# Two attention layers over one sparse graph: the adjacency turned into 8-bit floats by the transfers that load it

## The reference

```python
h = relu(layernorm(x))                          # x: 8192 x 128 f32
e = (h @ Ws) @ (h @ Wt).T                       # 8192 x 8192 scores
alpha = softmax(where(adj > 0, e, -9e15))       # adj: 8192 x 8192 int32, 0 or 1
x = x + alpha @ (h @ Wc)
h = relu(layernorm(x)); Wh = h @ W1
e = leaky_relu(s1[:, None] + s2[None, :], 0.2)  # s1 = Wh @ a1, s2 = Wh @ a2
x = x + elu(softmax(where(adj > 0, e, -9e15)) @ Wh)
```

## Time and profile before

| | |
|---|---|
| median of three runs | 1405.4 us |
| span of the profiled execution (its own time is not given beside it) | 1402.6 us |
| busy, share of the span | PE 91%, VectorE 89%, ScalarE 73%, GpSimd 2% |
| moved by DMA | 363.10 MB, of which the adjacency 268 MB |
| chain that ended last | PE 46%, DMA 18% (all of it the adjacency), VectorE 16%, "issue" 12% |

### The profile page before, as it was taken

One profiled execution on the slowest core, in us unless ns is written; L12 is line 12 of the kernel. 1 busy time (PEld: TensorE's weight loads), 2 busy tenths in 40 slices (PEclk: granted clock), 3 DMA queues, 4 the chain that ended last, 5 costly groups with the idle time before them and its releaser, 6 DMA issues.

```text
span 1402.6 us, 76097 instructions
## 1 busy us (share of the span) xinstructions
PE 1276.6 (91%) x31819; PEld 1131.9 (81%) x31947; DVE 1250.6 (89%) x2323; ACT 1024.8 (73%) x2036; POOL 32.3 (2%) x75
## 2 busy tenths in 40 slices
PE   5867899999999999999999999989899999999996
PEld 3656788888888888878878888877799999999995
DVE  8877799999999999989999999847899999999996
ACT  5755576767667677667676666748789999999994
POOL 2200000000000000000000000013000000000000
PEclk9979899999999999999999999999899999999998
DMA  6678899999999999999999999531134244334322
GB/s 249 248 266 287 280 345 369 370 381 368 368 391 357 377 378 366 383 380 341 382 378 361 376 374 374 223 114 55 56 108 121 81 124 123 108 94 123 117 85 72
DMA packets 104081, 363.10 MB, mean 259 GB/s; under 512 B 11520, under 2 KB 36352, under 8 KB 70144
## 3 DMA queue, kind: packets, MB, share of 16 engines
q1 hardware_dynamic: 103936, 361.02, 71.2%
HBM read 319.03 MB, written 41.94 MB: 257 GB/s over the span
## 4 chain that ended last, share of the span: by engine, by line
PE 46%; DMA 18%; DVE 16%; issue 12%; ACT 5%; SPq 1%; DVEq 1%; ACTq 0%; POOL 0%; POOLq 0%
DMA arena<-in_adjB 18%; PE ps L883 16%; PE ps L857 9%; DVE arena L1490 5%; PE ps L769 4%; DVE arena L1465 4%; PE ps L764 3%; PE ps L737 3%; DVE mx L1499 2%; ACT arena L1132 2%; PE ps L790 2%; PE ps L725 2%; PE ps L763 1%; PE ps L664 1%; SPq L434 1%
## 5 line engine op out<-in xcount | busy, mean ns | idle before, releaser
L790 PE MATMUL ps<-arena 128*128 128x129 f32 x2048 | 249.0, 280 | 0.4 <-issue 0.4
L1118 ACT ACTIVATE arena<-ps 128x512 f32<-128x512 f32 x256 | 153.2, 598 | 129.8 <-PE ps L737 129.8
L883 PE MATMUL ps<-arena 128*128 128x129 f32 x2048 | 245.1, 278 | 0.4 <-issue 0.4
L790 PEld LDWEIGHTS ps<-arena 128*128 128x128 f32 x2048 | 240.6, 196 | 0.6 <-issue 0.6
L1465 DVE TENSOR_SCALAR arena<-arena 128x2048 fp8e4<-128x2048 int32 x192 | 234.9, 1224 | 3.5 <-PE ps L752 1.5
L883 PEld LDWEIGHTS ps<-arena 128*128 128x128 f32 x2048 | 236.8, 194 | 0.5 <-issue 0.5
L1708 DVE TENSOR_SCALAR arena<-arena 128x128 f32<-128x128 f32 x768 | 202.4, 339 | 19.5 <-issue 14.3
L1112 ACT ACTIVATE arena<-ps 128x512 f16<-128x512 f32 x256 | 153.9, 601 | 52.5 <-PE ps L725 52.3
L769 PEld LDWEIGHTS ps<-arena 128*128 128x128 f16 x2048 | 137.5, 99 | 62.0 <-issue 2.2
L1499 DVE TENSOR_REDUCE mx<-ps 128x1 f32<-128x1024 f32 x128 | 155.7, 1216 | 29.9 <-PE ps L769 29.3
L737 PE MATMUL ps<-arena 128*32 128x128 f16 x8192 | 165.3, 223 | 16.5 <-issue 10.7
(11 more groups left out here) (165 smaller groups left out, 1400.4 us busy)
## 6 DMA issues: line engine op xcount, KB each, us to landing
arena<-in_adjB SPq DMA_DIRECT2D x256, 1024.0 KB, 7.3
sel_pick<-arena SPq DMA_DIRECT2D x64, 256.0 KB, 9.6
sel<-arena SPq DMA_DIRECT2D x64, 256.0 KB, 9.5
arena<-sel_pick SPq DMA_DIRECT2D x64, 256.0 KB, 3.8
arena<-sel SPq DMA_DIRECT2D x64, 256.0 KB, 2.8
arena<-in_xB SPq DMA_DIRECT2D x4, 1024.0 KB, 6.1
x_t<-in_x SPq DMA_DIRECT2D x64, 64.0 KB, 8.0
x_mid<-y_t SPq DMA_DIRECT2D x64, 64.0 KB, 8.3
```

The costliest lines, as they stand in the source:

```text
L790: last = nc.tensor.matmul(pv_ps, p_T[:, s * P:(s + 1) * P], v_sel[:, b, s, :], start=False, stop=(s == SB - 1), skip_group_check=True)
L883: last = nc.tensor.matmul(xv_ps[b], w_msk[:, b, s, :], x1_sel[:, b, s, 0:VW], start=False, stop=(s == SB - 1), skip_group_check=True)
```

## The change

The loads of the adjacency leave SyncE and go to GpSimd's queue, as two transfers of 2 MB a tile whose destination is an 8-bit float, so that the DMA engines turn int32 0 or 1 into 0.0 or 1.0. They land directly in mask buffers: four for the first four tiles, which are loaded during the first preparation (the first before any row is normalised, once `x` has landed), two for all later ones. The conversions go. The maximum over a tile is taken in two halves and compared with zero. The mask is gathered in four quarters of 16 matmuls with 128 columns of 8 bits; ScalarE subtracts 1 at the eviction, so an edge is 0 and no edge -1, and the product of ones goes. `indicate`, `place` and `prefix` move by about a step: the second half of `indicate` and `place` to the next step's first part, `prefix` behind the gathering of keys and values, and half of `pick_mask` of tile `e` to the end of the step. The rows of layer 0 stay on chip in `y_rows` and serve as `x_all[1]`; the store to `x_mid` stays, the load of 4 MB goes. Two limits are added to the final check.

```diff
+        y_rows = part(ADJ, N).rearrange("p (t d) -> p t d", d=D)
+        MASK_AT = (MASK, MASK + 2048, ADJ + 4096, ADJ + 6144)
+        mask_8 = [part(at, 2048, F8).rearrange("p (b n) -> p b n", n=P) for at in MASK_AT]
+        mask_u = [part(at, 2048, U32).rearrange("p (b w) -> p b w", w=P // 4) for at in MASK_AT]
@@ block.sync
-            def load_chunk(t, c):
-
-                if c < 3:
-                    wait(sp, conv_done, t * 3 + (c - 2))
-                else:
-                    wait(sp, conv_act, t)
-                rows = adjB[bass.ds(t, 1), c, :, :, :].rearrange("o p b n -> p (o b) n")
-                sp.dma_start(adj_st[:, c, :, :], rows).then_inc(adj_in[c], 16)
...
-                    load_rows(x_midB, 1, range(3))
...
-            load_rows(x_midB, 1, (3,))
@@ block.gpsimd
+            def load_half(t, h):
+
+                if t >= 4:
+                    last = t - 2 if t >= 6 else t - 4
+                    pool.wait_ge(mg_done, last * 4 + (2 * h + 2))
+                landed = adj_early if 2 <= t < 4 else adj_in
+                pool.dma_start(mask_8[t if t < 4 else t % 2][:, 2 * h * QCH:(2 * h + 2) * QCH, :].rearrange(
+                    "p (c b) n -> p c (b n)", c=2), adjB[t, 2 * h:2 * h + 2, :, :, :].rearrange("c p b n -> p c (b n)")
+                               ).then_inc(landed[t % 2][h], 16)
+
+            pool.wait_ge(xall_in[3], 16)
+            for h in range(2):
+                load_half(0, h)
+            for G in range(PREP):
+                make_h(G, G % 2, 0)
+                if G < 12 and G % 2:
+                    load_half(1 + G // 4, G % 4 // 2)
+            for t in range(4, TILES):
+                for h in range(2):
+                    load_half(t, h)
+            for G in range(PREP):
+                make_h(G, G % 2, 1)
@@ block.tensor
             def prefix(t, dst):
 
                 pe.wait_ge(ind_ready, t + 1)
-                wait(pe, m_evac, t * 2 - 2)
+                if dst is pre_ps:
+                    wait(pe, m_evac, t * 4)
...
+            def pick_mask(t, b, q):
+
+                if q == 0:
+                    pe.wait_ge(pick_ready, t + 1)
+                wait(pe, m_evac, t * 4 + q)
                 settle()
+                mask = mask_8[t if isinstance(t, int) and t < 4 else b]
+                for s in range(4):
                     for j in range(QB):
+                        k = (q * 4 + s) * QB + j
+                        last = nc.tensor.matmul(mg_ps[j * SLOT:(j + 1) * SLOT, s * P:(s + 1) * P],
+                                                pick[:, b, k, :], mask[:, k, :],
...
             def scores(t, b, q):
...
-                nc.tensor.matmul(dst, ones_b[:, :], negc, start=True, stop=False, skip_group_check=True)
-                nc.tensor.matmul(dst, off_i[q // 3], m_sel8[:, b, 4 * q:4 * q + 4, :].rearrange("p s n -> p (s n)"),
-                                 start=False, stop=False, skip_group_check=True)
+                nc.tensor.matmul(dst, off_i, m_sel8[:, b, 4 * q:4 * q + 4, :].rearrange("p s n -> p (s n)"),
+                                 start=True, stop=False, skip_group_check=True)
@@ tile_step of TensorE
-                if within(i, EARLY + 1, TILES + 1):
-                    prefix(i - 1, pre_ps)
...
                     pick_values(a, b, 0)
+                if within(i, EARLY + 1, TILES + 1):
+                    prefix(e, pre_ps)
                 if there(i, 4):
                     for g in range(4):
                         weigh(d, b, g)
...
                     scores(a, b, 0)
                     pick_values(a, b, 1)
+                if there(i, 1):
+                    pick_mask(e, cb, 0)
+                if there(i, 2):
                     scores(a, b, 1)
                 if there(i, 1):
-                    pick_keys(i - 1, cb, 0)
+                    pick_keys(e, cb, 0)
+                    pick_mask(e, cb, 1)
@@ block.scalar
+            def take_mask(t, b, q):
+
+                act.wait_ge(mg_done, t * 4 + (q + 1))
+                if q == 0:
+                    wait(act, m_out[b], (t - b) * 8)
+                act.sem_inc(evac_settled, 1)
+                nc.scalar.activation(m_sel8[:, b, 4 * q:4 * q + 4, :].rearrange("p s n -> p (s n)"), mg_ps,
+                                     ACT.Copy, bias=-1.0, saturate=False).then_inc(m_evac, 1)
...
-            def convert(t, b):
-
-                act.wait_ge(adj_in[3], t * 16 + 16)
...
@@ block.vector
-            def convert(t, b, c):
...
+            def indicate(t, b, h):
+
+                if isinstance(t, int) and t < 4:
+                    dve.wait_ge((adj_in if t < 2 else adj_early)[b][h], 16)
+                else:
+                    dve.wait_ge(adj_in[b][h], (t - b) * 8)
+                at = slice(2 * h * QCH, (2 * h + 2) * QCH)
+                mask = mask_u[t if isinstance(t, int) and t < 4 else b]
+                nc.vector.reduce_max(ind_raw[:, at], mask[:, at, :], AX_X).then_inc(ind_max, 1)
+                if h == 1:
+                    dve.wait_ge(ind_max, t * 2 + 2)
+                    nc.vector.tensor_scalar(ind[:, :], ind_raw, 0.0, None, ALU.is_gt).then_inc(ind_ready, 1)
@@ tile_step of VectorE
                 if there(i, 3):
                     spread_maximum(c)
-                if fresh:
-                    convert(i, b, 0)
+                if within(i, EARLY + 1, TILES + 1):
+                    indicate(e, 1 - b, 1)
                 if there(i, 3):
                     maximum(c)
...
+                if within(i, EARLY + 1, TILES + 1):
+                    place(e, pre_ps)
                 if there(i, 1):
                     make_pick(e, 1 - b)
...
                 if there(i, 2):
                     part_maximum(a, 0)
-                if fresh:
-                    place(i, pre_ps)
+                if within(i, EARLY, TILES):
+                    indicate(i, b, 0)
                 if there(i, 2):
                     part_maximum(a, 1)
```

More of the change, by code:

```diff
@@ L14 @@
 I32 = mybir.dt.int32
+U32 = mybir.dt.uint32
 ALU = mybir.AluOpType
@@ L44 @@
 BENT = (6, 7)
-NO_EDGES = struct.unpack("<f", bytes([0xB0] * 4))[0]
-NO_EDGES_ACT = struct.unpack("<f", bytes([0xB8] * 4))[0]
+TOP_LIMIT = float(2 ** 50)
 def gnn_kernel(nc, x, xB, adj, adjB, Ws, Wt, Wc, W1, a1, out, x_mid, sel, sel_pick):
@@ L98, in gnn_kernel @@
         assert VS + 2 * SB * VW <= PT and END <= TOP
-        negc = part(TOP + 2048, 256, BF16)
+        ind_raw = part(TOP + 2048, NB)
+        row_max = part(TOP + 2048 + NB, NB)
         mx_b = part(TOP + 2304, P)
@@ L105, in gnn_kernel @@
         tri = part(TOP + 2688, P // 2, F16)
-        off_i = [part(at, P // 2, BF16) for at in (TOP + 2752, END + 200)]
-        bare = part(END + 264, NB)
+        off_i = part(TOP + 2752, P // 2, BF16)
         ones_b = part(TOP + 2816, P // 2, BF16)
@@ L110, in gnn_kernel @@
         slots = part(TOP + 2912, SLOT // 2, F16)
-        ind_raw = part(TOP + 2928, NB)
         ind = part(TOP + 2992, NB // 2, F16)
@@ L256, in gnn_kernel @@
         decided_redo = sem("decided_redo")
-        adj_in = [sem(f"adj_in{c}") for c in range(4)]
-        conv_done = sem("conv_done")
-        conv_act = sem("conv_act")
-        conv_settled = sem("conv_settled")
+        adj_in = [[sem(f"adj_in{b}_{h}") for h in range(2)] for b in range(2)]
+        adj_early = [[sem(f"adj_early{b}_{h}") for h in range(2)] for b in range(2)]
+        evac_settled = sem("evac_settled")
         ind_max = sem("ind_max")
@@ L457, in tile_io @@
             def tile_io(i, b):
-                if within(i, 0, TILES - 1):
-                    for c in range(4):
-                        load_chunk(i + 1, c)
                 if there(i, 1):
@@ L481, in _ @@
             load_rows(xB, 0, (1, 2, 3))
-            for c in range(4):
-                load_chunk(0, c)
             load_x(0, 0)
@@ L601, in make_h @@
                 last.then_inc(h_pool, 1)
-            for mode in range(2):
-                for G in range(PREP):
-                    make_h(G, G % 2, mode)
+            def load_half(t, h):
[18 more added lines that the diff above has]
+                make_h(G, G % 2, 1)
             def mask(tau, m):
@@ L740, in pick_values @@
                 last.then_inc(vg_done, 1)
-            def pick_mask(t, b, h):
-                wait(pe, m_evac, t * 2 + h)
-                if h == 0:
-                    pe.wait_ge(posx_ready, min(t + 2, TILES) if isinstance(t, int) else t + 2)
+            def pick_mask(t, b, q):
+                if q == 0:
+                    pe.wait_ge(pick_ready, t + 1)
+                wait(pe, m_evac, t * 4 + q)
                 settle()
-                half = P // 2
-                for s in range(8):
+                mask = mask_8[t if isinstance(t, int) and t < 4 else b]
+                for s in range(4):
                     for j in range(QB):
-                        k = (h * 8 + s) * QB + j
-                        last = nc.tensor.matmul(mg_ps[j * SLOT:(j + 1) * SLOT, s * half:(s + 1) * half],
```

(11 more changed lines are left out.)

137 lines of the change are left out of this document (51 added, 86 removed).

## The result

The changed kernel takes 1387.7 us (median of 4 runs, 1382.2 to 1388.8) against 1406.2 for the kernel before (4 runs beside it). The ratio is 0.988, 95% interval 0.984 to 0.993: faster by 1.2%, 18.5 us, where 62 were forecast. The profiled execution spans 1386.1 us. Of the 16.5 us of span, 8.7 are these 53 tiles, 5.0 the first eight, 5.8 the last two, and the start and the end give back 3.

The account below looks back on a forecast made before the run. DMA was taken to bound the sweep at 13.0 us a tile, TensorE next at 95% of it. 1402.6 - 49 - 3 - 7 - 3 = 1341 us of span, so 1343 us; range 1318 to 1412.

Parts of the forecast that it names:

- DMA is the bound: Layer 0's sweep before the change: DMA engines, busy 0.98 at 369 GB/s, set the 13.0 us a tile.
- so I take under 10.0: Converting adjacency loads in the sweep: under 10.0 us a tile, 10.7 before, so that TensorE bounds.
- Reading decides: Rival, sweep: DMA time follows bytes read, adjacency keeps 10.7 us a tile, period stays; 1396 us, chance 0.19.
- the slow rival: Sweep: converting takes the DMA engines longer than copying; 1695 us at one and a half times today's 10.7; chance 0.21.
- TensorE's 11.7 us: TensorE's dense work a tile in the sweep after the change: 12.3 - 0.9 + 0.3 = 11.7 us.
- The gather of the mask: TensorE in the sweep: doubled columns at the same number of matmuls, +0.15 us twice, +0.3 a tile.
- The 12.3 of dense work: TensorE before the change, one sweep tile: 12.65 us from start to start, of which 0.34 is an idle gap.
- the new waits: TensorE in the sweep: `pick_mask` round trips, `prefix` and `indicate` waits, 0.4 us a tile, ends 0 and 1.3.
- The lead of the buffers: Sweep loads: each half tile is asked for about a period before it is needed, which covers GpSimd's issue.
- Preparation: First preparation: conversions and a wait gone, -6; GpSimd's wait for `x` and two issues, +3; net -3 us.
- First tiles: First seven tiles, before 200 us: 0.6 us each and shorter instruction-stream stalls, -7 us, ends 0 and -15.
- End of the sweep: The load of `x_mid` goes, with a 2.97 us issue stall at 919.36: -3 us, ends 0 and -4.

Follow-up runs that it names:

- The added store: The kernel before with each tile's gathered mask stored a second time, 256 KB more a tile: 1403.3 us, ratio 0.9998.
- the quarter-read pair: Kernel before (from the second tile) and changed kernel (adjacency as int8), each reading only a quarter of every adjacency row: 1359.1 us and 1357.6 us.
- finer requests: The changed kernel with four 1 MB converting transfers a tile for two of 2 MB, each issued once its own quarter was gathered: 1364.3 us, ratio 0.973.

## Why the prediction was wrong

Of the 0.9 us a tile that were forecast, 0.16 came. 0.4 of the rest is TensorE, whose floor is 12.5 us and not 12.1; 0.33 is the late landing of the halves.

**The reading of the bound** failed first. "DMA is the bound" rested on a share of 0.98 at 369 GB/s. The added store in the kernel before moved nothing (1403.3 for 1403.8 us). The evidence for a wait was sound: ScalarE did wait for its chunk. But it waited for a chunk that was asked for late (13.0 us are the turn of the fourth chunk). A share near 1 can't tell the two apart.

**The step "so I take under 10.0"** failed in what it said: the quarter of written bytes would relieve the transfers. Alone, 4.19 MB take the same time converted as plain (42.4 and 43.1 us for four times that), 10.6 us with the start of a stage in it; in the sweep, from 300 to 700 us, the packets of that queue took 89.4% of the 16 engines' time for 63 halves, 11.4 us a tile, where 10.7 were worked out for the plain ones. "Reading decides", given 0.19, had the mechanism of the conversion right, and its 1396 us was nearer than 1343; it was wrong in that the period was held by throughput. Nothing that converts too slowly was seen; the slow rival (0.21) is out.

**TensorE's 11.7 us** was 12.5. The product of ones was priced right: 0.22 us each, 0.88 for four in the kernel before with a quarter of the bytes. The gather of the mask was mis-sized, +0.6 for +0.3: 32 matmuls of 128 columns were priced at 0.49 us, the row of the values' gather, but cut into two groups of 16 they take 0.67. And the new order was put at nothing: what a gather costs depends on its neighbours, and the gathers of keys, of values and the scores together took 0.3 us more (+0.45, -0.27, +0.13) though their own instructions are the same. So -0.9 + 0.6 + 0.3 is 0, and the quarter-read pair shows it: 12.45 us the median tile before, 12.46 after. The 12.3 of dense work were a little low too. Of the new waits the round trips through the mask's bank cost next to nothing (L750 idle 4.3 us in 31 tiles, 0.1 a tile), under the 0.4 taken, `prefix` hardly more.

**The lead of the buffers** stands in the prediction as "cover", "about a period before it is needed". It was taken for cover without being added up. That is where the difference between 12.5 and 12.84 lies: the second half landed 12.1 us after its issue, and with the 13.4 us behind its landing the turn had next to no slack. 54 x 0.33 = 18 us were lost there; finer requests gave back 17 in the steady tiles and 23 in all.

**Outside the sweep.** Preparation: +1.2 at the first transpose instead of -3; the wait for `x` on GpSimd cost 4.3 (first product at 17.33 for 13.00), and undoing it gave 3.4. First tiles: -5.0 for -7. End of the sweep: -5.8 for -3; the 2.97 us stall at 919.36 is gone, with the 4 MB load that ran there. That was not tried by itself. GpSimd's issue: 0.71 us for the 1 us taken, harmless as work.

Sum: 53 steady tiles gave 8.7 us for 49 x 53/54 = 48; the rest gave 7.8 for 13. The lower end of the range does not come out of the prediction's own ends, which give 1310 us and not 1318; nothing hangs on it.

## What to carry to other kernels

When a DMA share stands near 1 and an engine waits for a load, ask which of two things is short, bytes or lead: add a useless transfer (if nothing moves, there is room), or split the load and ask for each part as soon as its own space is free. In a double buffer count the turn, from issue to landing to the last reader to the next issue, leave out what the landed data lie waiting, and divide by the tiles that it serves; the period can't fall below that number, whatever the transfer's share of the engines. The part to look at is the one that lands last and lies least. And cost a group of short matmuls from start to start, in the order in which it will stand, between the neighbours that it will have, with the bank that it needs and the engine that empties it.

## What was not expected of the hardware

- A transfer that converts int32 to 8-bit float reads at the rate of a plain one: 16.8 MB in 42.4 us for 43.1. Writing a quarter of the bytes saves nothing, and int8 to 8-bit float takes 22.3 us where int8 as it is takes 15.6.
- In the sweep a 1 MB chunk issued from GpSimd landed 0.9 us later than from SyncE (8.2 and 7.3 us), though throughput is equal (43.1 and 42.8 us for 16.8 MB). The kernel with one staging area lost 0.63 us a tile by the move.
- Sixteen matmuls that gather keys hold TensorE for 0.40 us before scores, for 0.69 before a gather of the mask, and for 0.48 there when other products were added.
- 256 KB more a tile, stored beside loads that show a DMA share of 0.98 to 1.04, cost 0 to 4 us in 64 tiles.
- After a wait of 2.95 us TensorE's clock was granted at 0.56, and 32 products took 6.40 us for 3.79; behind 12 of 13 waits of 2.0 to 3.7 us it was low, and they took 5.4 to 6.7.
